# A cross-attention over 12544 keys on one Trainium2 core: each placement of key rows spread over 32 partitions, and the maxima of the first five steps moved

## What is computed

```
q = layernorm(x) @ Wq.T + bq ; k = ctx @ Wk.T + bk ; v = ctx @ Wv.T + bv   # ctx: 12544 x 256
attn = softmax(q k.T * 0.25) per head (16 heads, HEAD_DIM 16) ; x = x + (attn v) @ Wo.T + bo
x = x + linear_attention(layernorm(x))          # 128 rows
x = x + block(layernorm(x))                     # causal attention and 8 experts, top 2, 128 rows
```

## Time and profile before

| | us |
|---|---|
| median of 3 runs (lowest, highest) | 540.59 (539.01, 543.27) |
| the profiled execution | 538.97 |
| its span, from first to last instruction seen | 537.2 |

### The profile page before, as it was taken

How to read it: one execution, slowest core, us unless ns; L and a number is a source line. 1 busy time by engine, 2 the same in 40 slices (tenths; PEclk the granted TensorE clock), 3 DMA queues, 4 the chain that set the end, 5 groups by cost and what they waited for, 6 DMA issues and landing times.

```text
span 537.2 us, 19592 instructions
## 1 busy us (share of the span) xinstructions
PE 507.8 (95%) x8408; PEld 461.1 (86%) x8408; DVE 386.2 (72%) x712; ACT 346.8 (65%) x688; POOL 90.2 (17%) x75
## 2 busy tenths in 40 slices
PE   7998999999999999999999999999999989776997
PEld 7887889999999999999999999999877878565886
DVE  5488778777877878777787877777774347937574
ACT  3422678787787887878788788777766720162563
POOL 5761101111101101111110110110000000052000
PEclk9999999999999999999999999999999999868899
DMA  6999978969898896988789698877790079800000
GB/s 193 153 157 166 141 137 129 142 124 144 137 135 145 123 157 113 151 140 126 146 116 153 123 148 138 129 128 96 115 294 5 3 255 377 308 1 1 2 0 10
DMA packets 44631, 70.65 MB, mean 132 GB/s; under 512 B 6785, under 2 KB 15105, under 8 KB 44417
## 3 DMA queue, kind: packets, MB, share of 16 engines
q1 hardware_dynamic: 44304, 69.02, 69.6%
q10 hardware_dynamic: 240, 0.39, 0.5%
HBM read 30.53 MB, written 0.13 MB: 57 GB/s over the span
## 4 chain that ended last, share of the span: by engine, by line
PE 85%; DVE 10%; ACT 2%; issue 2%; POOL 0%; DMA 0%; SPq 0%; DVEq 0%; ACTq 0%
PE weighted L759 17%; PE scores L742 15%; PE bank L620 13%; PE bank L638 13%; PE maxima L665 11%; PE scores L1039 3%; PE maxima L1023 2%; DVE stepmax L1136 2%; PE scores L767 2%; DVE stepmax L1128 2%; PE bank L1023 2%; PE scores L788 1%; PE bank L567 1%; PE bank L587 1%; PE scores L1032 1%
## 5 line engine op out<-in xcount | busy, mean ns | idle before, releaser
L1136 DVE TENSOR_REDUCE stepmax<-maxima 128x2 f32<-128x512 f32 x344 | 225.5, 688 | 74.8 <-PE maxima L665 70.1
L433 ACT ACTIVATE probs<-scores 128x512 f32<-128x512 f32 x376 | 204.3, 596 | 75.8 <-PE scores L742 75.2
L620 PE MATMUL bank<-cparts,wk 64*128 64x256 f32 x1104 | 177.0, 287 | 1.0 <-DVE kst L1119 0.9
L638 PE MATMUL bank<-wv,cparts 64*128 64x256 f32 x1104 | 171.5, 287 | 0.5
L620 PEld LDWEIGHTS bank<-cparts,wk 64*128 64x128 f32 x1104 | 145.5, 186 | 2.2 <-DVE kst L1119 1.8
L638 PEld LDWEIGHTS bank<-wv,cparts 64*128 64x128 f32 x1104 | 145.5, 186 | 1.5 <-PE bank L638 1.5
L665 PE MATMUL maxima<-kT,qM 64*128 64x256 f32 x688 | 111.9, 305 | 2.8 <-DVE stepmax L1136 1.2
L742 PE MATMUL scores<-qmat,kT 64*128 64x128 f32 x1504 | 113.0, 265 | 1.3 <-DMA qmat<-maxT 0.6
L347 POOL TENSOR_TENSOR cparts<-ctxT,cparts 128x512 fp32r<-128x512 f32 x49 | 63.1, 1287 | 287.9 <-ACT cparts L393 287.9
L742 PEld LDWEIGHTS scores<-qmat,kT 64*128 64x128 f32 x1504 | 103.5, 187 | 3.9 <-ACT probs L433 1.7
L759 PE MATMUL weighted<-probs,val 128*17 128x128 f32 x3136 | 96.5, 273 | 0.0
(11 more groups left out here) (224 smaller groups left out, 427.2 us busy)
## 6 DMA issues: line engine op xcount, KB each, us to landing
kT<-kst SPq DMA_DIRECT2D x291, 128.0 KB, 4.7
ctxT<-in_ctxT SPq DMA_DIRECT2D x49, 256.0 KB, 6.9
w<-in_w SPq DMA_DIRECT2D x24, 512.0 KB, 10.0
bias<-in_biases SPq DMA_DIRECT2D x1, 1024.0 KB, 8.0
kT<-kst ACTq DMA_DIRECT2D x3, 128.0 KB, 4.9
qmat<-maxT SPq DMA_DIRECT2D x24, 8.0 KB
w_xk<-in_w_xk SPq DMA_DIRECT2D x1, 256.0 KB, 2.6
w_xq<-in_w_xq SPq DMA_DIRECT2D x1, 256.0 KB, 3.8
```

Source lines behind the costliest of these rows:

```text
L433: act.activation(probs[k % PROBS][:, :, :], late_bank[score_banks(k - q % 2)[q % 2]][:, :].rearrange("p (h q) -> p h q", q=P), ACT.Exp).th ...
L620: last = pe.matmul(k_bank[:, cols], wk[rows, pw, c, t * P:(t + 1) * P], cparts[n % 2][rows, pc, c, :], start=not swapped and i == 0, stop= ...
L638: last = pe.matmul(v_bank[:, cols], cparts[n % 2][rows, pc, c, j * P:(j + 1) * P], wv[rows, pw, c, :], start=not swapped and i == 0, stop= ...
L1136: dve.tensor_reduce(heads[:, 2 * m:2 * m + 2], bank[:, :].rearrange("p (i k) -> p i k", i=2), AX_X, ALU.max).then_inc(S["mx_read"], 1)
```

## The change

A helper `key_row(a, seg)` gives the first row of a segment. Segments 0 and 1 are interleaved in rows 64a to 64a + 31 (even and odd rows), segments 2 and 3 in rows 64a + 32 to 64a + 63. Each placement DMA still moves 16 rows of 8 KB, now to every second of 32 partitions. The queries follow: `qparts` gets the index order (pair, half, upper or lower 32, element, even or odd), so that VectorE and GpSimd write it with a step of two elements. `keys_place` has segments in the outer loop and halves in the inner one. In the steps t < 5 the third unit of maxima stands behind 5 rounds in place of 6 and the fourth behind 11 in place of 16.

```diff
+def key_row(a, seg):
+    return 64 * a + 2 * HD * (seg // 2) + seg % 2
...
-        qparts = place("qparts", [P, PAIRS, 2, 4, HD], F32R)
+        qparts = place("qparts", [P, PAIRS, 2, 2, HD, 2], F32R)
...
-                for a in range(2 if n else 1):
-                    for seg, part in enumerate((0, 1, 0)):
-                        row = 64 * a + HD * seg
-                        sp.dma_start(kT[row:row + HD, n % RING, :, :].bitcast(F32).rearrange("d (i t) k -> d i (t k)", t=2),
+                for seg, part in enumerate((0, 1, 0)):
+                    for a in range(2 if n else 1):
+                        row = key_row(a, seg)
+                        sp.dma_start(kT[row:row + 2 * HD:2, n % RING, :, :].bitcast(F32).rearrange("d (i t) k -> d i (t k)", t=2),
                                      kst[n % 2][64 * a:64 * a + 64, part, :].bitcast(F32)
...
-                    row = 64 * a + 3 * HD
-                    sp.dma_start(qmat[b % 2][row:row + 2, :, :].bitcast(F32),
+                    row = key_row(a, 3)
+                    sp.dma_start(qmat[b % 2][row:row + 4:2, :, :].bitcast(F32),
...
-            pool.memset(qparts[:, :, :, 3, :].bitcast(F32), 0.0)
+            pool.memset(qparts[:, :, :, 1, :, 1].bitcast(F32), 0.0)
...
-                    row = 64 + HD * seg
-                    act.dma_start(kT[row:row + HD, 0, :, :].bitcast(F32).rearrange("d (i t) k -> d i (t k)", t=2),
+                    row = key_row(1, seg)
+                    act.dma_start(kT[row:row + 2 * HD:2, 0, :, :].bitcast(F32).rearrange("d (i t) k -> d i (t k)", t=2),
...
-                    project_both(t + LEAD, False, 0, 6)
+                    project_both(t + LEAD, False, 0, 5)
                     early_maxima(t, 2)
-                    project_both(t + LEAD, False, 6, 12)
-                    project_both(t + LEAD, True, 0, 4)
+                    project_both(t + LEAD, False, 5, 11)
                     early_maxima(t, 3)
-                    project_both(t + LEAD, True, 4, 12)
+                    project_both(t + LEAD, False, 11, 12)
+                    project_both(t + LEAD, True, 0, 12)
...
-                last = dve.scalar_tensor_tensor(qparts[:, :, :, seg, :].rearrange("q p a d -> q (p a) d"),
+                last = dve.scalar_tensor_tensor(qparts[:, :, :, 0, :, seg].rearrange("q p a d -> q (p a) d"),
...
-            dve.scalar_tensor_tensor(qparts[:, :, :, 2, :], q4, SCALE, qparts[:, :, :, 0, :].bitcast(F32),
+            dve.scalar_tensor_tensor(qparts[:, :, :, 1, :, 0], q4, SCALE, qparts[:, :, :, 0, :, 0].bitcast(F32),
```

More of the change, by code:

```diff
@@ L810, in _ @@
                     last = pe.transpose(mx_bank[i][:, p * P:(p + 1) * P].bitcast(F32R),
-                                        qparts[:, PAIRS // 2 * i + p, :, :, :].rearrange("q a s d -> q (a s d)"),
+                                        qparts[:, PAIRS // 2 * i + p, :, :, :, :].rearrange("q a u d s -> q (a u d s)"),
                                         ident_r[:, :])
```

## The result

The changed kernel takes 534.72 us (median of 4 runs, 534.11 to 535.92) against 540.11 (4 runs): ratio 0.9892, 95% interval 0.9852 to 0.9932. The profiled execution took 535.16 us with a span of 533.4, 3.8 us less than before. The forecast was 538.0 in a range of 535.0 to 541.3: the gain is about twice the one summed up, and the median lies 0.28 us under the range. (Runs more than 1.5% above the fastest of their kernel in the same round are left out of all comparisons.)

A forecast was written before the change was run, and what follows sets the result against it. The prediction took TensorE's own work to bound the middle, so the change could touch only what lies ahead of about 75 us. Terms of 0.59, 0.58 and 1.38 sum to 2.55 us: from 540.59 to 538.0, range 535.0 to 541.3.

The forecast's parts named there:

- Price of a placement: DMA engines: a 128 KB placement falls from 0.98 us of full share to 0.49, bounds 0.38 and 0.98.
- second rival: Placements stay as dear, paced by source or count of destination partitions; only the maxima's gain is left: 540.0 us, chance 0.1.
- Term 1: Early steps: full DMA engines make PE wait for placements in steps 2 and 3; 0.59 us goes.
- term 2: Steps 0 to 4: third and fourth units of maxima come sooner; 0.58 us, 0.50 of it behind step 4.
- Term 3: Step 6: PE's 1.16 us stop, taken as an instruction fetch late behind placements, goes; 1.38 us.
- Term 4: Small edits, such as strided `qparts` writes at the start, and sooner placements in the middle steps: zero gain.
- fourth rival: Full queues cost unprofiled runs more than the profiled one, and DVE leads the early steps: 534.2 us, chance 0.09.

The follow-up runs named there:

- e2: The changed kernel with the old order of the maxima in the first steps; 536.70 us, ratio 0.9938 to the kernel before.
- e1: The kernel before, run again with no edit; 540.47 us, ratio 1.0013.
- e12: The kernel before, run again with no edit for a third trace; its steps 0 to 5 take 44.61 us.
- e9: The changed kernel plus three useless 128 KB DMAs onto 16 adjacent partitions in each of steps 0 to 35; 538.26 us, 0.9972 of the kernel before.
- e14: The changed kernel plus four useless 128 KB DMAs onto 16 adjacent partitions in each of steps 8 to 37; 539.83 us, 0.9977 of the kernel before.
- e13: The changed kernel plus three useless 128 KB DMAs onto 16 adjacent partitions in steps 0 to 7 only; 538.46 us, 0.9936 of the kernel before.

## Why the prediction was right and wrong

**Price of a placement.** Right in kind and near in size: 0.41 us, forecast 0.49, bounds 0.38 and 0.98. The second rival (the cost stays) is out.

**Term 1 (0.59) and term 2 (0.58).** Right together: 1.17 forecast for steps 0 to 5, 1.15 measured. Steps 2 and 3 fell to 6.31 and 6.32 us. Apart, the placements are worth 0.68 us (43.29 and e2's 42.61, forecast 0.59) and the order of the maxima 0.47 (e2's 42.61 and 42.14, forecast 0.58). Term 1's 0.59 is one trace's: in e1 and e12 step 2 takes 6.33 and 6.30 us and only step 3 is long, 6.71 and 6.64. DVE's idle time ahead of unit 0 became 0.75 us, forecast 0.5. On PE the fourth unit lies 2.14 us ahead of the next step's maxima (26.34 to 28.48), before 1.20 (27.62 to 28.82): it came 0.94 us sooner, not 0.60, as the swap of the halves no longer lies ahead of it. That cost nothing, PE's end bound as said.

**Term 3 (1.38).** The size was right in the two traces (9.22 to 7.84 us), and it goes with the old rows, but not as one stop in step 6: three traces of the kernel before have 1.5, 0.65 and 2.8 us of it at other places, 1.7 on the mean. The reason given, fetches behind full queues, is not shown; e9 speaks against it.

**Term 4 (nothing).** Right: the middle steps are 7.84 us and 260.00 of 260.00 as before; the start is not later.

**The step that failed** is the last one of the sum: "with the same distance the median becomes 538.04". The forecast median was 3.32 us too high. 1.26 of it is in the profiled execution, 535.16 and not the 536.42 summed up: it lies in the start, one middle step and the end, for which the sum has nothing. The other 2.06 is the distance between the profiled execution and the median: before, the profiled execution lay 1.62 us below the median, and this was carried over; after, it lies 0.44 us above it. The prediction took the waits of one trace of before for those of its median run, each at its own length and nothing more, and that trace happened to be one without a fall of the clock ahead of the end.

What stands in its place is the table of the traces. Over the three of before, step 0 starts at 23.77 us on the mean, steps 0 to 5 take 44.20 and the stops 1.7; over the two of after it is 22.26, 42.14 and nothing. The differences are 1.5, 2.1 and 1.7 us, 5.2 in all, where the spans differ by 4.4, so 0.9 is lost again behind the steps; the medians differ by 5.0. Of the 2.1 in the first steps, 1.17 was in the sum, and the rest goes with the clock's fall at 60 to 66. The 1.5 of the start goes with the fall at 12 to 18, which the changed kernel's program has too (e14), so that it stays open how much of it the change took away and how much is which runs were traced. With three traces and two this is a sketch and no measurement of each part.

The fourth rival had this in half: "full queues cost each unprofiled run more than the profiled one" (1.62 us). It was put together with a second condition (DVE leads the early steps), which is false, at 0.09 for both. Its 534.2 us is near the 534.72 measured by luck only. Apart, the first condition deserved far more, since the three runs shown before already differed by 4.3 us in a kernel whose plain steps repeat to 0.01 us. The range's lower end, 535.0, was too high for the same reason: it allowed for scatter about a distance that was itself wrong. The changed kernel's 12 runs scatter over 2.8 us, the first three of before over 4.3.

## What to carry to other kernels

Judge a DMA within SBUF by its share of the DMA engines against a transfer that touches all partitions at full rate: here 0.98 against 0.38 us for the same 128 KB gave the fault away, and a stride of two partitions mended it at no cost, though the queues were no bound of the long middle. When the runs of a kernel differ by more than its regular steps can, ask which waits the spread comes from before carrying a saving over to the median, and take a second trace: a wait that goes can take a fall of TensorE's clock in other executions with it. A run's mean clock doesn't tell where the clock fell; only stretches of a trace do. Full queues delayed the regular steps only at the start, where each step had to have its placement at once, so look at shares by stage.

## What the runs showed of the hardware that was not expected

- The DMA cost of 128 KB from 64 partitions fell from 0.98 to 0.41 us of full share by spreading 16 destination rows from 16 adjacent partitions to every second of 32; every fourth of 64 is no cheaper (share 0.41 both).
- PE can stop for 0.4 to 1.9 us in a stretch without any wait, at places that change from run to run (69, 135, 356 us), in three of five traces with the first layout and once, for 0.4 us, in e14; a share of 0.83 with other traffic didn't bring it back.
- After a stretch with PE busy 1.11 of 2 us (e12), or 4.11 of 6 (e13), the mean granted clock was 0.72 over the next 6 us and 0.57 over the next 4. The same program shows it in some executions and not in others: of three traces of the kernel before, two have two falls each ahead of 72 us, and one has none ahead of the kernel's end, with a mean clock of 0.981 against 0.981 and 0.987.
